# Matmuls of an identity that nobody reads, placed where TensorE has no work in the sorts, the edge softmax and the first scatter pass

## The reference

```python
edge_index = jnp.stack([src, dst])
h = jnp.maximum(_layernorm(x, axis=-1), 0.0)
x = x + _L0_gnn_ref(h, edge_index, ...)   # softmax over the edges of a node, sum, two-layer MLP
h = jnp.maximum(_layernorm(x, axis=-1), 0.0)
x = x + _L1_gnn_ref(h, ..., edge_index)   # edge MLP with two batch norms, sum per node
h = jnp.maximum(_layernorm(x, axis=-1), 0.0)
x = x + _L2_gnn_ref(h, edge_index, edge_attr_3, ...)   # two spline convolutions
h = jnp.maximum(_layernorm(x, axis=-1), 0.0)
x = x + _L3_gnn_ref(h, edge_attr_8, ..., edge_index)   # three message layers
```

## Time and profile before

| | us |
|---|---|
| median of 3 runs | 9387.17 |
| lowest and highest of the runs | 9379.37 and 9951.77 |
| the profiled execution | 9400.52 |
| its span, first to last instruction | 9398.8 |
| PE busy in it | 2821.1 (30%) |
| DVE busy | 4174.4 (44%) |
| ACT busy | 1297.4 (14%) |
| POOL busy | 5190.7 (55%) |

### The profile page before, as it was taken

One profiled execution on the slowest core, in us unless ns is written; L12 is line 12 of the kernel. 1 busy time (PEld: TensorE's weight loads), 2 busy tenths in 40 slices (PEclk: granted clock), 3 DMA queues, 4 the chain that ended last, 5 costly groups with the idle time before them and its releaser, 6 DMA issues. The chain is left out here.

```text
span 9398.8 us, 39754 instructions
## 1 busy us (share of the span) xinstructions
PE 2821.1 (30%) x8711; PEld 1768.9 (19%) x8711; DVE 4174.4 (44%) x7182; ACT 1297.4 (14%) x2213; POOL 5190.7 (55%) x5107
## 2 busy tenths in 40 slices
PE   0000000000232310127663444277333144245222
PEld 0000000000231100003221333155222123123111
DVE  4367448970024440104543677677655411312311
ACT  0000001000011110016551000011033111011000
POOL 5744741887436637770335665266266366366366
PEclk9965555555555555558876666677655555555555
DMA  1100100001133201111111111122134222222111
GB/s 41 26 20 16 25 15 6 19 18 36 44 102 48 38 16 23 21 16 33 41 38 34 33 35 34 41 32 32 46 64 66 59 33 34 48 31 35 51 31 28
DMA packets 364620, 331.83 MB, mean 35 GB/s; under 512 B 115499, under 2 KB 339968, under 8 KB 363379
## 3 DMA queue, kind: packets, MB, share of 16 engines
q0 software_dynamic: 163072, 77.69, 9.5%
q1 hardware_dynamic: 199282, 249.37, 8.1%
q10 hardware_dynamic: 2048, 2.41, 0.1%
HBM read 173.11 MB, written 158.67 MB: 35 GB/s over the span
## 5 line engine op out<-in xcount | busy, mean ns | idle before, releaser
L917 POOL DMA_INDIRECT c_ring<-tab,QB x784 | 758.7, 968 | 732.2 <-POOLq L102 306.6
L917 POOL DMA_INDIRECT g_ring<-tab,QB x784 | 749.7, 956 | 621.3 <-issue 234.4
L917 POOL DMA_INDIRECT l_ring<-in_x_dram,a_own x392 | 528.6, 1348 | 386.9 <-POOLq L102 267.7
L1489 PE MATMUL c_psU<-spline,c_hzT 96*128 96x288 f32 x1568 | 547.8, 497 | 190.8 <-DVE c_V L1453 145.2
L917 POOL DMA_INDIRECT l_ring<-agg_tab,QA x392 | 393.5, 1004 | 363.3 <-POOLq L102 205.6
L917 POOL DMA_INDIRECT nodes_ring<-nodes,b_own x256 | 254.1, 993 | 594.7 <-DMA x2d_lin<-nodes_ring 516.6
L917 POOL DMA_INDIRECT H<-xe_tab,idx_a x392 | 402.1, 1026 | 320.9 <-DVEq L788 200.6
L2035 POOL DMA_INDIRECT out_dram<-out_rowr,out_idxr x392 | 386.4, 986 | 284.7 <-DVE out_idxr L2079 149.1
L917 POOL DMA_INDIRECT c_ring<-nodes,b_other x392 | 397.7, 1015 | 262.5 <-DVEq L1586 137.8
L1366 POOL DMA_INDIRECT nodes<-l1s_rowr,a_out x392 | 386.2, 985 | 264.7 <-DVE l1s_rowr L1382 145.5
L917 POOL DMA_INDIRECT sort_ring<-in_x_dram,sort_raw x392 | 402.3, 1026 | 121.3 <-issue 120.3
(11 more groups left out here) (473 smaller groups left out, 8052.4 us busy)
## 6 DMA issues: line engine op xcount, KB each, us to landing
tab<-M SPq DMA_DIRECT2D x5, 6272.0 KB
nodes<-l_xout SPq DMA_DIRECT2D x40, 322.3 KB
nodes_x<-nodes SPq DMA_DIRECT2D x50, 257.8 KB
c_din<-dst_lin SPq DMA_DIRECT2D x98, 128.0 KB
c_ring<-tab,QB POOLq DMA_INDIRECT x784
dst_lin<-c_yd SPq DMA_DIRECT2D x98, 128.0 KB
g_din<-dst_lin SPq DMA_DIRECT2D x98, 128.0 KB
g_ring<-tab,QB POOLq DMA_INDIRECT x784
```

The lines of the kernel that those rows point to most:

```text
L917: pool.indirect_dma_start(out=ring[:, at + j, :], out_offset=None, in_=table, in_offset=bass.IndirectOffsetOnAxis(ap=idx[:, w:w + 1], axis ...
L1489: ins = pe.matmul(self.psU[i % 2][:, t, 0:288], self.hzT[c % 2][:, (2 * i + t) * P:(2 * i + t + 1) * P], w[:, :, :].rearrange("p j o -> p ...
```

## The change

TensorE gets extra matmuls. Class Spare multiplies the identity by the identity, spread over as many 128-column blocks as its PSUM tile has: 512 columns in the sort and in l1s, 256 in l0 (there the tile is the unused half of `psA[0]`). The product goes to a PSUM place that nobody reads, and no semaphore is waited for or incremented. `spare.run(pe, n)` issues n of them. PE takes its instructions in order, so a transpose or carry that stands behind them starts when they are through, whether DVE has asked long before or not.

```diff
+class Spare:
+    def __init__(self, g, ps):
+        self.g, self.ps = g, ps
+        self.n = ps.shape[1] // P
+
+    def run(self, pe, n):
+        for i in range(n):
+            pe.matmul(self.ps.rearrange("p (t f) -> p t f", f=P), self.g.ident[:, :], over(self.g.ident[:, :], 1, self.n),
+                      start=True, stop=True)
...
         for lv in range(7):
             pe.wait_ge(self.across, self.next("pe", "across"))
             self.turn_columns(pe, self.X[0], self.psC, lists, self.crossed)
+            self.spare.run(pe, 55 if lv == 6 and ride else lists * (lv + 1))
             pe.wait_ge(self.along, self.next("pe", "along"))
             self.turn_rows(pe, self.C[(lv + 1) % 2], self.psT, lists, self.turned)
+            if lv < 6:
+                self.spare.run(pe, 11 * lists)
...
+        spare.run(pe, 105)
         pe.wait_ge(self.ask, 1)
...
+        spare.run(pe, 60)
         pe.wait_ge(self.ask, 2)
...
+        spare.run(pe, 105)
         pe.wait_ge(self.ask, 3)
...
+        spare.run(pe, 60)
         pe.wait_ge(self.ask, 5)
         n.turn_columns(pe, n.XW[1], self.grid, G2, self.crossed, P)
+        spare.run(pe, 38)
         pe.wait_ge(self.ask, 6)
...
         def _(pe):
+            net.spare.run(pe, 160)
             net.tensor(pe, 2, True)
             join.tensor(pe)
+            net.spare.run(pe, 140)
             net.tensor(pe, 2, False)
+            net.spare.run(pe, 105)
             net.tensor(pe, 1, False)
...
+            spare = Spare(g, psA[0][:, 256:512])
             for q in range(D // F):
+                spare.run(pe, 140)
                 carry_pe(g, pe, c, q * KG)
+                spare.run(pe, 140)
                 carry_pe(g, pe, c, q * KG + 2)
+            spare.run(pe, 200)
             carry_pe(g, pe, cb, 0, back=True)
+            spare.run(pe, 200)
...
             carry_pe(g, pe, c, 0)
+            spare.run(pe, 900)
```

More of the change, by code:

```diff
@@ L255, in __init__ @@
         self.psC = ph.ps("psC", (P, GQ, P))
+        self.spare = Spare(g, ph.ps("spare")[:, :])
         self.psT, self.psW = ph.ps("psT", (P, G2, SF)), ph.ps("psW", (P, G2, SF))
@@ L408, in tensor @@
     def tensor(self, pe):
-        n, ident = self.net, self.g.ident
+        n, ident, spare = self.net, self.g.ident, self.net.spare
+        spare.run(pe, 105)
         pe.wait_ge(self.ask, 1)
@@ L1345, in layer1_rest @@
         c = carry_tiles(ph, D)
+        spare = Spare(g, ph.ps("spare")[:, :])
         rowr = [ph.sb(f"rowr{i}", [P, CH, D + 1]) for i in range(NR)]
```

## The result

The changed kernel takes 11257.3 us (median of four, 11249.8 to 11264.9), the kernel before beside it 9394.6: a ratio of 1.199, 95% interval 1.197 to 1.201, slower by 1863 us. One of the four runs of the kernel before took 9951.8 us; it is counted as a slow one and left out of the ratio. Slower was forecast, but by 255 us. The range of 9500 to 9800 was missed by 1460.

The account below looks back on a forecast made before the run. Sorts were taken as bound by PE increments arriving late, l1s by POOL, join and third sort by a DVE-PE chain. Overruns of +381 us less 126 given back make +255 on 9387.17: 9642 us, range 9500 to 9800.

Parts of the forecast that it names:

- What one new matmul costs.: All stretches: a 512-column new matmul is two records at 0.429 us, so 0.858 us at 2.4 GHz, half for 256 columns.
- The rivals on the price: Each new matmul costs 0.43 us, total down to about 9085 (chance 0.10), or is dearer, 9870 and above (0.05).
- dearer matmul: Long bursts or repeated columns raise the matmul's price; l1s adds 100 us per 0.11 us, 9870 and above; chance 0.05.
- Late increments: In the sorts, PE's finished turns reach DVE late while POOL gathers; DVE waits 8.84 and 16.64 us.
- The give-back of 126 us: Sorts: only row-turn increments come in time, idle ahead of column turns shrinks to 18.9 us; -49 a sort, -28 seventh levels.
- the bound of 236: Sorts: most that can come back if all PE increments arrive at once, -97 in each sort plus 42 for seventh levels.
- l0 +26: In l0, DVE's chain ends some 198 us later, but an MLP standstill covers all except 5.6 chunks of 4.6 us.
- l1s +236: In l1s, 900 new matmuls take 772.2 us, outlasting POOL's last scatter, so the barrier waits 236 us for PE.
- the load at 2244.89: In l0, the MLP stands still until 2244.89 us for a load behind POOL's gathers, covering most of DVE's delay.
- all of them go: Rival: every late PE increment in the sorts vanishes, six levels take 160 us, total 9532, slower by 1.5%; chance 0.18.
- The clock falls: Rival: the clock drops in so long a burst, making matmuls dearer; 9870 us and above; chance 0.05 shared with repeated columns.
- The 0.52 us: Skill-based estimate for a 512-column new matmul, with which nearly every block would fit its gap; set aside for the trace's 0.858.

Follow-up runs that it names:

- the narrow ones: Kernel before with only the 900 new matmuls of l1s, each of 128 columns instead of 512; 9582 us, +183.

## Why the prediction was right or wrong, point by point

- **The step that failed: "What one new matmul costs."** I took 0.858 us from a stretch of nodes in which POOL was idle and used it in stretches in which POOL sends without pause, where a new matmul took 5.60 us. The same trace had 5.60 us for the same shape 200 us earlier, beside POOL's gathers. In l1s the rows of line 238 span 1207 us where I had forecast 770. The rivals on the price reached from 0.43 us up to "each 0.11 us adds 100", and the chance of a dearer matmul, 0.05, was put on "nothing in the trace speaks for it". Those rows did.
- **"Late increments": seen, read wrongly.** I took them for a delay that costs nothing while PE has nothing to do, and expected new work behind them to bring them forward. They go by the number of PE's pairs, so new work lengthens them. One division would have told: 44.8 us for 16 pairs, 39.2 for 14, 5.60 for two. And c2, my case without them, was no match for the sorts: POOL sends eight transfers there in 10 us and then stops for 2 to 3 us (6103 to 6598 us of the trace), while in the sort it sends 392 without a stop.
- **The give-back of 126 us** came out larger, above even the bound of 236, and did not matter. The first sort's six levels took 159.2 us (651.26 to 810.48) in place of 257.1, the second's 171.1, and what lies behind these six another 89 less: 272 in all. But only because PE had first worked off its blocks until POOL was through: the first question is answered 450 us later than before, and the second sort begins another 479 later. 450 + 479 - 272 is, but for a rounding, the 656 of the stage.
- **"l0 +26" and "l1s +236"** became +537 and +663 by the same step. The claim that the l0 blocks hide behind the load at 2244.89 fell with it: PE ended its blocks at 3656, 1411 us into the stage, and not 670 (2260 - 1590).
- **Where there is no slow pace, the unit price holds.** (The kernel before on kind 2 is read from the run with transposes in l1s, whose other stages are its own.) On kind 2 l1s is 239 us longer (805.8 against 566.6), forecast 236; l0 29, forecast 26; 105 matmuls take 90.29 us, forecast 90.1; six levels 159.2, forecast 160 for "all of them go"; the four inner blocks of the join overrun by 18.2, 31.2, 17.7 and 12.0, forecast 18.1, 31.2, 17.4 and 11.8. The stage sort is 239 longer and not 109 less a give-back, since DVE asks earlier there, so that the blocks ahead of the first question and of the second sort overrun by 52 and 41 and not by 8 and 19, and each level grows by 5.5. The unit price was sound for PE alone; what it lacked was the condition. The total would have been missed there too, +507 against +255: with no slow pace there are no late increments to give anything back, and DVE asks earlier.
- **"The clock falls"** was no cause: it follows the idle time between the pairs. That the higher clock buys next to nothing agrees with the trace: nodes is 17 us shorter and all that lies outside the five stages 7.
- **The 0.52 us.** The Trainium skill (TensorE: Matmul & The Clock Gate, Back-to-back issue gap; four passes for float32 by FP8 and Floating Point Precision, TensorE Precision Notes) had led to an estimate of 0.52 us a matmul; even on kind 2 the trace has 0.86, and the measurement decides.

## What the runs showed of the hardware that I had not expected

On chips of kind 1 a run of indirect transfers of POOL without a pause takes PE and DVE down to one pair of instructions in 2.80 us on average, whatever their size. It sets in 30 to 39 us after the run's start with the new matmuls (68 to 123 pairs of PE). With the narrow ones, which come nearly four times as densely, the first gaps stand after 9 us and some 80 pairs and the full 2.80 us after some 20; with light load it takes some 50 us. So it goes rather by how many instructions are through than by time. Groups of 24 transfers with 6.2 us between them keep it away. Where it is there, stops of 2 us do not end it; under light load stops of 6.8 and 7.3 us did, and behind a whole run with PE dense it lasted 22 to 25 us more. Two instructions in 2.80 us hold for PE and DVE each, also at the same time.

In the end it reaches POOL itself. In l1s of the changed kernel the first hundred transfers stand 1.29 us apart, the last hundred 1.39:

```profile
4701.17 0.98 POOL L1400 DMA_INDIRECT nodes<-l1s_rowr,a_out  x1 [0.30 <-issue]
4702.46 0.98 POOL L1400 DMA_INDIRECT nodes<-l1s_rowr,a_out  x1 [0.30 <-issue]
...
5116.31 1.10 POOL L1400 DMA_INDIRECT nodes<-l1s_rowr,a_out  x1 [0.30 <-issue]
5117.72 1.09 POOL L1400 DMA_INDIRECT nodes<-l1s_rowr,a_out  x1 [0.30 <-issue]
```

One instruction in 1.40 us is the pace of PE and DVE too. With PE idle in l1s (the kernel before) and on kind 2 the last hundred stand 1.29 apart.

The kernel before takes 9379 to 9402 us on one kind of chip (and once 9952) and 7803 to 7833 on the other. By stages it is sort 1514 against 1058, l0 1118 against 911, nodes 1080 against 731. l1s, where PE has next to nothing to do and POOL sends 392 transfers, takes 566 us on both.

What it is stays open. Starts fall on a raster of 0.70 us, and 2.80 is four of its steps. The Trainium skill (NOTIFIC — the notification-queue block, The AWS profiler on NQ 0) says that the profiler records the start and the end of every instruction; two instructions make four records. The Trainium skill (NOTIFIC — the notification-queue block, Overflow: three behaviours, one of which stalls the engine) says that the block's internal pipeline pushes back on those who send records rather than lose one. By these, 0.70 us would be the time of one record of one engine, and the slow pace would be a cost of recording on chips where that path is slow. The sizes agree with that, POOL's 1.40 us a transfer too, and nothing here shows it: every execution of this study was recorded, so no time without recording stands against it. One run speaks against its simplest form. In l1s with pauses PE got through 1411 pairs in 605 us, by this count 5644 records at 0.11 us each, beside POOL's transfers on kind 1. So 0.70 us is not what a record costs as such; something has to fill up first, and why POOL's transfers fill it is not known. A slow fetch of instructions is a rival that no run tried; from 107 to 622 us of the changed kernel's trace only 6 packets of the instruction queues were moved. Whether memsets of POOL in place of its transfers would bring the slow pace is open too; 6 us of them did not.

## What to carry to other kernels

Before an engine's idle time is filled, look at the pace at which that engine gets through instructions in that very stretch, start to start, and not at its busy time or at a price from a stretch with other neighbours; where it gets through one pair every 2.8 us, idle time is not free time. Divide a wait by the number of instructions beside it: where several give the same quotient (44.8 for 16, 39.2 for 14), look for a rate and not for a latency. And since breaking up POOL's runs of indirect transfers gained 601 us on one kind of chip and lost 318 on the other, measure such a change on more than one chip.
